# Depthwise taps of three image groups summed in two PSUM banks, half a map per VectorE instruction, TensorE's taps first

## What is computed

```python
x = x + L0(gn(x))    # mixture of experts on 2x2 patches, top 2 of 8
x = x + L1(gn(x))    # deformable 3x3 convolution: four corners gathered per tap
x = x + L2(gn(x))    # state space layer, 16 delays, gated unit, layer norm
x = x + L3(gn(x))    # depthwise 7x7, layer norm over channels, MLP
```

```python
y = jax.lax.conv_general_dilated(x, dw_w, window_strides=(1, 1), padding=[(3, 3), (3, 3)],
                                 feature_group_count=x.shape[1], ...)
y = y + dw_b[None, :, None, None]
```

## Time and profile before

| | |
|---|---|
| median of 3 runs | 1698.12 us (1697.15 to 1698.41) |
| the profiled execution, its own time | 1698.67 us |
| its span in the profile | 1696.9 us |
| TensorE matmul busy | 1339.8 us (79%) |
| VectorE busy | 1006.1 us (59%) |
| ScalarE busy | 541.9 us (32%) |
| GpSimd busy, all of its work | 1180.7 us (70%) |
| the chain that ended last, by engine | PE 37%, POOL 25%, DVE 20%, issue 10% |

### The profile page before, as it was taken

One profiled execution on the slowest core, in us unless ns is written; L12 is line 12 of the kernel. 1 busy time (PEld: TensorE's weight loads), 2 busy tenths in 40 slices (PEclk: granted clock), 3 DMA queues, 4 the chain that ended last, 5 costly groups with the idle time before them and its releaser, 6 DMA issues.

```text
span 1696.9 us, 13775 instructions
## 1 busy us (share of the span) xinstructions
PE 1339.8 (79%) x4164; PEld 611.3 (36%) x4164; DVE 1006.1 (59%) x1809; ACT 541.9 (32%) x870; POOL 1180.7 (70%) x1187
## 2 busy tenths in 40 slices
PE   8778566999849958879969848789849644898797
PEld 7543233444324413324334313334224211343345
DVE  4546765544662479943655588845433794445785
ACT  2122212323332331243423412342413304244345
POOL 1477777756777777777777778777777777777700
PEclk9889877999969979989979979989869876899899
DMA  7233223421322222322332223322221112222000
GB/s 254 64 82 84 79 66 84 118 61 56 92 78 73 65 57 77 90 75 56 86 97 59 62 62 84 92 64 70 61 76 53 50 53 59 81 64 68 22 10 16
DMA packets 109609, 123.06 MB, mean 73 GB/s; under 512 B 49952, under 2 KB 85856, under 8 KB 109408
## 3 DMA queue, kind: packets, MB, share of 16 engines
q0 software_dynamic: 36864, 75.57, 15.8%
q1 hardware_dynamic: 71712, 43.40, 10.0%
q10 hardware_dynamic: 960, 3.21, 0.5%
HBM read 101.89 MB, written 9.01 MB: 65 GB/s over the span
## 4 chain that ended last, share of the span: by engine, by line
PE 37%; POOL 25%; DVE 20%; issue 10%; ACT 5%; DMA 2%; SPq 1%; DVEq 0%; POOLq 0%; ACTq 0%
POOL gt L1042 25%; PE bank L1991 7%; PE bank L2004 6%; DVE rb L1742 5%; PE bank L1941 4%; PE bank L1905 4%; PE bank L1901 3%; PE bank L1915 3%; DVE gt L1626 3%; PE bank L1974 2%; DVE he L1524 1%; PE bank L2027 1%; DVE gt L1628 1%; PE bank L2048 1%; PE bank L1805 1%
## 5 line engine op out<-in xcount | busy, mean ns | idle before, releaser
L1042 POOL DMA_INDIRECT gt<-corner_table,idx x1152 | 1155.8, 1003 | 422.3 <-issue 347.3
L1991 PE MATMUL bank<-u,wk 128*128 128x512 f32 x512 | 240.4, 614 | 3.7 <-DMA u<-sqb 3.7
L2004 PE MATMUL bank<-yg,wts 128*128 128x512 f32 x512 | 234.3, 602 | 0.4 <-DVE rb L1682 0.2
L1626 DVE TENSOR_TENSOR gt<-gt,bank 128x1152 f32<-128x1152 f32 x128 | 172.6, 1349 | 88.2 <-DMA gt<-corner_table,idx 87.1
L1905 PE MATMUL bank<-xg,w_sb 128*128 128x512 f32 (+1 forms) x256 | 135.3, 612 | 45.1 <-DVE xg L1515 23.3
L1961 PE MATMUL bank<-cst,sm 128*128 128x128 f32 x384 | 75.9, 313 | 118.1 <-DVE sm L1634 117.9
L1668 DVE SCALAR_TENSOR_TENSOR tg<-tg,ae 128x512 f32<-128x512 f32 x64 | 44.1, 692 | 198.2 <-ACT ae L1218 198.2
L1742 DVE SCALAR_TENSOR_TENSOR rb<-xp,par,rb 128x1024 f32<-128x1024 f32 x124 | 155.0, 1291 | 0.0
L1991 PEld LDWEIGHTS bank<-u,wk 128*128 128x128 f32 x512 | 97.3, 197 | 121.7 <-issue 114.7
L1524 DVE SCALAR_TENSOR_TENSOR he<-he,bank 128x512 f32<-128x512 f32 (+1 forms) x128 | 83.0, 651 | 92.0 <-PE bank L1905 88.8
L2004 PEld LDWEIGHTS bank<-yg,wts 128*128 128x128 f32 x512 | 95.2, 192 | 111.5 <-issue 109.4
(11 more groups left out here) (283 smaller groups left out, 1512.5 us busy)
## 6 DMA issues: line engine op xcount, KB each, us to landing
gt<-corner_table,idx POOLq DMA_INDIRECT x1152
tb<-gate_of_token SPq DMA_DIRECT2D x56, 256.0 KB, 4.9
u<-sqb SPq DMA_DIRECT2D x48, 128.0 KB, 2.8
corner_table<-tb SPq DMA_DIRECT2D x36, 128.0 KB, 2.7
w_sb<-w ACTq DMA_DIRECT2D x6, 512.0 KB, 7.1
xp<-x_patch SPq DMA_DIRECT2D x4, 512.0 KB, 4.4
X<-x SPq DMA_DIRECT2D x1, 1536.0 KB, 9.2
out<-X SPq DMA_DIRECT2D x6, 256.0 KB, 2.2
```

Of the source, the lines that this page charges most:

```text
L1042: pool.indirect_dma_start(gt[:, t % GRING, k].rearrange("p a c -> p (a c)"), None, corners, bass.IndirectOffsetOnAxis(ap=idx[s % 2][:, j, ...
L1626: ch.then(tt(rows, rows, share.unsqueeze(2).to_broadcast([P, 4 * KK, C]), ALU.mult))
L1991: op = mm(psum[b][:, :], wk[:, t, d], u4[:, g, at:at + HALF], start=t == 0, stop=t == JJ - 1 and n > 0)
L2004: op = mm(psum[B2.bank(*name)][:, :], w_glu[:, k, col + d * P:col + (d + 1) * P], yg[:, c % 2, k], start=k == 0, stop=k == NB2 - 1)
```

## The change

For the first three groups (`s < FOLDED`, which is 3) TensorE's taps come first. VectorE then waits until the two banks hold TensorE's sums, and adds its own taps straight into the banks, in two instructions of 512 pixels each: input `xp3` in SBUF, the sum read from a bank and written to it. `l3_sum` is then one pass over each bank that adds the bias and writes the sum to SBUF. Nothing else is changed.

```diff
@@ order_l3
     done = 0
+    if s < FOLDED:
+        parts += [("pe_tap", s, mine + i) for i in range(PE_TAPS[s])]
+        done = PE_TAPS[s]
     for t in range(mine):
         parts.append(("tap", s, t))
         while done < (t + 1) * PE_TAPS[s] // mine:
@@ VectorE
+            def tap_in_banks(s, t):
+                if t == 0:
+                    for n in halves(s):
+                        B2.filled(dve, "tap", s, n)
+                for n in halves(s):
+                    y = psum[B2.bank("tap", s, n)][:, :].rearrange("p (h w) -> p h w", w=W)
+                    if t:
+                        ch.wait(last[n])
+                    last[n] = ch.did(stt(out=y, in0=window(s, t, n), scalar=prm("dw")[:, t:t + 1], in1=y, op0=ALU.mult, op1=ALU.add))
+
             def tap(s, t):
+                if s < FOLDED:
+                    return tap_in_banks(s, t)
                 win = window(s, t)
...
                 if t == 0:
-                    if s < FOLDED:
-                        dve.wait_ge(S["xp3_ready"], s + 1)
-                    elif s < PARTS - 1:
+                    if s < PARTS - 1:
@@ l3_sum
                 y = ya_(s)
+                if s < FOLDED:
+                    for n in halves(s):
+                        ch.wait(last[n])
+                        b = B2.bank("tap", s, n)
+                        ts(y[:, 0, n * HALF:(n + 1) * HALF], psum[b][:, :], prm("dw_b"), None, ALU.add).then_inc(free[b], 1)
+                    return
                 ch.wait()
```

## The result

The changed kernel takes 1716.99 us (median of six runs, 1713.80 to 1720.31), the kernel before 1697.63 (1695.62 to 1698.67): a ratio of 1.0113, with a 95% interval of 1.0098 to 1.0128. That is 19 us more. The profiled execution took 1713.80, the fastest of the six, and the one of the kernel before 1698.67, the slowest of its six. The traces come from these two, so they show about 15 of the 19 us.

A forecast was written before the change was run, and what follows sets the result against it. From 401 to 1586 us GpSimd's gathers were taken to set the pace. The three groups, +10.2, -10.2 and +23.4, summed to +23.4 us: 1722.1 in the profiled execution's terms, 1721.5 as a median, range 1703 to 1737.

The forecast's parts named there:

- A tap costs 1.33 us: VectorE in the first three groups: two half-size bank operations make a tap of 1.33 us, against 1.21 or 1.24 before.
- rival 3: An operation that reads and writes a bank is dearer, up to 1.49 us a tap: 19 us more, 1741; chance 0.12.
- Relief of 13.2, 12.8 and 0 us: Gathers of groups one, two and three: time no longer lost waiting for taps with two SBUF inputs.
- Rival 4: Gathers wait for the new taps too, so the second group gives nothing: 10.2 us more, 1731; chance 0.05.
- First group +10.2: Up to tile 54: dearer taps 6.2 us plus a new wait for TensorE 4.0, all passed on to GpSimd.
- Second group -10.2: Tiles 76 to 86: gathers 12.8 us earlier, less 2.6 because dearer taps use up the 17.4 of slack.
- Third group +23.4: The deciding term: addition to X 17.0 us late, taps 12.1 more, mean 27.9 later, less 4.5 slack at tile 112.
- The milder path: Third group: the sample of tile 109, just ahead of l3_sum, has 8.7 us of slack against 29.1 of lateness.
- rival 1: Third group: TensorE's taps don't hold VectorE up, so it costs 6.4 us and the run takes 1704; chance 0.12.
- rival 2: Faster: the gathers' relief comes through everywhere, 26.0 us less, 1672; chance 0.10.
- rival 5: Whole kernel: small shifts cancel and the time ends within 0.2% of the kernel before; chance 0.06.
- The signs: Profile after: gathers 0.95 us, half-taps 0.66 apart, tile 54 some 10 later, waits mostly tiles 104-112, VectorE idle some 24.

## Why the prediction was right, step by step

It said 1721.5 us, slower; 1716.99 was measured, inside its range, and the decisive term was the right one. The medians flatter it. In terms of the profiled execution it said 1722.1 and 1713.80 came: the trace moved by 15.1 us where the sum had 23.4.

- **A tap costs 1.33 us**: right. Sixteen halves take 10.62 us, so they start (10.62 - 0.75) / 15 = 0.66 apart, 1.32 a tap. An operation that reads and writes a bank costs what the half-size one in SBUF costs, and rival 3 is out; so is a price for the bank. The Trainium skill (VectorE: DVE Perf Modes, section The TRN2 errata) asks for 62 cycles more an operation, by an estimate from them 0.065 us a half, and the trace has none of it.
- **Relief of 13.2, 12.8 and 0 us**: right in size (93.38 - 80.34 = 13.0 and 92.94 - 80.38 = 12.6) and in its reason: no gather waits for an operation with one input in a bank. What it left out is a second way to most of the same relief, which the change takes as well: halves with both inputs in SBUF give 8.7 to 10.0 of the second group's 12.9. Rival 4, that gathers wait for the new taps too, is out.
- **First group +10.2**: it was +8.5 (716.50 to 725.01). The wait is 5.65 us rather than 4.0: TensorE's twelve records took 8.08 us, the first 3.6 of them at a granted clock of 0.50 (below). VectorE's work grew by 5.5 rather than 6.2 (94.03 busy us before, 99.55 now, from 615.90 up to the sample of tile 50). What the sum lacked is that 2.6 us of VectorE's other idle time went into it (6.3 before, 3.6 now beside the wait): 5.65 + 5.5 - 2.6 = 8.5. The wait is a matter of the order as much as of the banks: the kernel with the order alone loses 4.1 here.
- **Second group -10.2**: it was -12.1 (from +5.9 at tile 76 to -6.1 at tile 86). The slack was not used up: the sample of tile 82 ends at 1094.16, 1.1 us before GpSimd needs it, where the sum had it 2.6 late. VectorE's idle time took up the rest there too.
- **Third group +23.4**: it was +21.2. With GpSimd 7.1 us ahead at tile 107, the addition to `X` is 1359.32 - 1349.15 + 7.1 = 17.3 later (17.0 in the sum), and `l3_sum` 1426.14 - 1404.08 + 7.1 = 29.2 (29.1 in the sum). What was off is the piece behind it, from `l3_sum` to the end of the sample of tile 112: 3.7 us shorter than before, not 1.2. TensorE's `dcn` in it took 3.75 us instead of 5.17, at another granted clock. The two stretches, before and after (busy us of PE, PEld, DVE, ACT, POOL, then the clock):

```profile
1429.60:1438.40 8.80, 7.94 (x23) 1.80 (x23) 0.00 (x0) 0.55 (x2) 6.67 (x8) 0.52 0.19 55
```

```profile
1450.40:1456.80 6.40, 5.58 (x23) 1.52 (x23) 0.00 (x0) 0.58 (x2) 4.88 (x6) 0.73 0.20 51
```

- **What the wording left out**: the text put the wait on the late `dcn` alone, with the sample behind it. That is the wait which ends last in the changed kernel, but VectorE's first tap has to wait for the same eleven taps of TensorE. With the `dcn` moved out of the way this second wait took over and the cost stayed; with seven taps in the gap it fell by 5 us. The sum was right since it counted the time until VectorE can start its taps.
- **The milder path**: the sample of tile 109 was to have 8.7 us of slack against 29.1, which is 20.4. GpSimd indeed waits at every tile from 108 to 113 and is 20.7 behind there; the chain behind `l3_sum` added only 0.5. That the clock was kinder there hardly showed for this reason.
- **The sum**: 8.5 - 12.1 + 21.2 = 17.6, where the prediction had 23.4. Between the groups GpSimd caught up 2.6 us (tiles 54 to 76) and 0.9 (tiles 86 to 107) that the sum did not expect, which leaves the 14.1 at tile 116 and 14.3 at tile 127 (1574.91 to 1589.23). The medians differ by 19.4, since the changed kernel's profiled execution lies 3.2 below its median and the other's 1.0 above. What the slower ones do differently no trace shows. That the forecast came within 4.5 us of the median is in this part luck.
- **Rivals 1, 2 and 5** did not come: VectorE was held up in the third group, and the relief came through in one of the two groups that had any.
- **The signs**: all came but one. Of the 52.4 us that GpSimd waits for samples, most was to lie between tiles 104 and 112. 24.5 lie ahead of tiles 108 to 116, and nearly as much, 23.0, ahead of tiles 51 to 54 in the first group: there the gathers' relief turned into waiting.

## What to carry to other kernels

An operation moved to the front of an in-order engine is paid for by whoever waits behind it: count the time until the waiting engine can start, and all that stands in its queue, not the one result that is late. Moving that one result out of the way can just uncover the next wait. A relief for the engine that sets the pace is worth something only where its suppliers have slack; here the same edit was worth 12 us in one group, cost 8.5 in another that had the same relief, and cost 21 in the third, which had none to gain. So a change that touches several places is to be tried place by place: the second group alone is 0.6% faster than the kernel before, all three together 1.1% slower.

## What the runs showed of the hardware that I had not expected

- With both inputs of the VectorE operations in SBUF, halving them took 8.7 to 10.0 us of 12.9 from 81 gathers, wherever the output went (82.92 and 84.25 us against 92.94). With one input in a bank the length doesn't count: no gather that started well inside the 1.35 us of L1626 took over 0.95.
- TensorE's taps take longer in a stretch that opens at the lower clock: twelve records at 0.43 us each at full clock are 5.2 us, and took 8.08 where the granted clock began at 0.50, TensorE's 1.2 GHz. The engine had been idle for 5.13 us before them. The changed kernel's two stretches (PE, PEld, DVE, ACT, POOL, clock):

```profile
613.40:617.00 3.60, 3.60 (x5) 1.53 (x6) 2.46 (x4) 1.40 (x2) 2.69 (x4) 0.50 0.18 54
617.00:621.40 4.40, 4.40 (x10) 1.88 (x9) 0.00 (x0) 0.00 (x0) 3.18 (x5) 0.81 0.17 46
```
